# Retention scores of a macaron block: fp32 matmuls on four 32-row groups instead of hi/lo fp32r pairs

## The reference, cut to what matters

```python
x = x + 0.5 * ffn(layernorm(x))          # x is 1 x 1024 x 256
x = x + attn(layernorm(x))
x = x + 0.5 * ffn(layernorm(x))
# ffn: y = (silu(h @ gate * gs) * (h @ up * us)) @ down * ds, weights rounded to fp8, inner width 768
# attn: 16 heads of 16
q, k, v = split(h @ w_qkv)
q, k = xpos(q), xpos(k)                  # x * cos + rotate_every_two(x) * sin
scores = q @ k.T * D ** -0.5 * mask      # mask[h, t, s] = gamma_h ** (t - s) for t >= s, else 0
y = scores @ v
y = (y - mean) / sqrt(var + eps) * gn_weight + gn_bias      # over each head's 16 columns
out = (silu(h @ w_g) * y) @ w_proj
```

## Time and profile before

| | |
|---|---|
| three runs, us | 187.33, 188.22, 187.22; median 187.33 |
| span of the profiled execution | 187.8 us (its own time is not given apart from the span) |
| PE | 171.6 us busy, 91% |
| DVE | 142.9 us, 76% |
| ACT | 104.5 us, 56% |
| POOL | 62.9 us, 34% |
| PE clock granted, mean | 0.960 of full speed (1.0 is 2.4 GHz, 0.5 is 1.2 GHz) |

### The profile page before, as it was taken

One profiled execution on the slowest core, in us unless ns is written; L12 is line 12 of the kernel. 1 busy time (PEld: TensorE's weight loads), 2 busy tenths in 40 slices (PEclk: granted clock), 3 DMA queues, 4 the chain that ended last, 5 costly groups with the idle time before them and its releaser, 6 DMA issues.

```text
span 187.8 us, 3246 instructions
## 1 busy us (share of the span) xinstructions
PE 171.6 (91%) x1091; PEld 131.9 (70%) x1091; DVE 142.9 (76%) x302; ACT 104.5 (56%) x202; POOL 62.9 (34%) x68
## 2 busy tenths in 40 slices
PE   6745999899899999998999999999999999799992
PEld 2223867688878775866687777867677887588882
DVE  2899589999745486667796968878799899636664
ACT  3164199767208448584939576674926763224710
POOL 3535363353825210124161605215263915000000
PEclk9985599999999999999999999999999999889998
DMA  5898004403000000000000000000000000011002
GB/s 172 276 332 293 5 2 143 191 3 113 0 0 3 0 0 3 0 0 2 3 0 0 3 0 0 3 3 2 0 3 0 0 0 0 3 56 58 0 17 98
DMA packets 6848, 8.41 MB, mean 45 GB/s; under 512 B 416, under 2 KB 5552, under 8 KB 6832
## 3 DMA queue, kind: packets, MB, share of 16 engines
q1 hardware_dynamic: 6832, 8.20, 12.9%
HBM read 7.15 MB, written 1.05 MB: 44 GB/s over the span
## 4 chain that ended last, share of the span: by engine, by line
PE 36%; POOL 8%; DVE 7%; issue 5%; ACT 4%; POOLq 0%; DVEq 0%; ACTq 0%
PE bank L1017 12%; POOL grstd L326 6%; PE bank L1044 3%; PE bank L1121 3%; PE bank L1184 3%; PE bank L1141 3%; PE bank L1097 3%; PE bank L1070 2%; ACT fhi L451 2%; DVE rot L740 1%; PE bank L1134 1%; PE bank L1084 1%; PE bank L1081 1%; PE bank L1166 1%; DVE fuse L685 1%
## 5 line engine op out<-in xcount | busy, mean ns | idle before, releaser
L1017 PE MATMUL bank<-hh,gate_r 128*128 128x512 f32 x96 | 30.3, 436 | 4.7 <-DVE hh L669 2.3
L1017 PE MATMUL bank<-hh,up_r 128*128 128x512 f32 x96 | 28.0, 415 | 0.0
L398 ACT ACTIVATE gact<-bank,vec 128x512 f32<-128x512 f32 x24 | 16.4, 684 | 17.0 <-PE bank L1017 16.9
L1017 PEld LDWEIGHTS bank<-hh,gate_r 128*128 128x128 f32 x96 | 17.9, 202 | 11.2 <-issue 4.3
L1044 PE MATMUL bank<-down_r,fhi 128*128 128x256 f32 x96 | 25.1, 298 | 0.3 <-DVE flo L693 0.3
L326 POOL TENSOR_TENSOR grstd<-gve,neg_half 128x16 f32<-128x16 f32 x8 | 23.4, 2928 | 0.7
L1044 PE MATMUL bank<-down_r,flo 128*128 128x256 f32 x96 | 23.5, 282 | 0.0
L1017 PEld LDWEIGHTS bank<-hh,up_r 128*128 128x128 f32 x96 | 19.3, 201 | 4.7
L748 DVE TENSOR_TENSOR sc<-bank,msk 128x512 f32<-128x512 f32 x32 | 21.3, 682 | 0.7 <-PE bank L1121 0.7
L685 DVE SCALAR_TENSOR_TENSOR fuse<-bank,vec,gact 128x512 f32<-128x512 f32 x24 | 17.9, 744 | 3.8 <-PE bank L1017 3.6
L302 POOL TENSOR_SCALAR ve<-mv 128x1 f32<-128x1 f32 (+2 forms) x13 | 4.2, 321 | 49.1 <-DVE mv L630 49.1
(11 more groups left out here) (85 smaller groups left out, 346.1 us busy)
## 6 DMA issues: line engine op xcount, KB each, us to landing
raw<-in_rotation SPq DMA_DIRECT2D x1, 1536.0 KB, 6.5
xt<-in_L_attn_x SPq DMA_DIRECT2D x2, 512.0 KB, 4.6
out<-xt SPq DMA_DIRECT2D x8, 128.0 KB, 1.7
raw<-in_L_ffn_down_w SPq DMA_DIRECT2D x2, 384.0 KB, 7.5
wqkv<-in_L_attn_w_qkv SPq DMA_DIRECT2D x1, 768.0 KB, 9.4
raw<-in_rotation SPq DMA_DIRECT2D x1, 512.0 KB, 3.3
raw<-in_L_ffn_gate_w SPq DMA_DIRECT2D x1, 384.0 KB, 6.3
raw<-in_L_ffn_up_w SPq DMA_DIRECT2D x1, 384.0 KB, 6.9
```

Of the source, the lines that this page charges most:

```text
L398: nc.scalar.activation(gact[:, j % 2, :], pairs[j // (NG * NI)][j % 2][0][:, :], ACT.Silu, scale=gate_col[:, i:i + 1]).then_inc(silu_done, 1)
L1017: mm = pe.matmul(dst[:, :], wr[m][:, k * I + i * P:k * I + (i + 1) * P], half[:, k, g % NG, :], start=(k == 0 and half is hhi), stop=(k == ...
```

## The change

Scores become fp32 matmuls. Rotated q and k are transposed once (four 128 x 128 transposes into one bank). Of the transposed tile each 32 partitions hold two heads, so the score matmuls of 32 rows each take k's 32 partitions as weights and two masked copies of q as the moving side; row group r writes into bank 3 + r, all heads of it side by side, and one mask call evicts a bank. The state is summed in SBUF (`kvm` masked by DVE, `add_state` on POOL) in two slots, so that `b_kv` shares a bank with y. `group_mean` to `group_norm`, `gated` and `project_out` are reordered, and the roots on POOL with them. The core of the diff:

```diff
-        turn = [(bank[0], bank[1])] * 3 + [(bank[3], bank[4])]
-        pairs = [[(bank[2], bank[3]), (bank[4], bank[5])], [(bank[2], bank[5]), (bank[0], bank[1])]]
+        turn = [(bank[0], bank[1])] * 2 + [(bank[1], bank[2]), (bank[5], bank[6])]
+        pairs = [[(bank[2], bank[3]), (bank[4], bank[5])], [(bank[3], bank[4]), (bank[1], bank[2])]]
+        b_y, b_kv, b_qk, b_vg = bank[0][:, 0:C], bank[0][:, C:2 * C], bank[1], bank[2]
+        b_sc, b_gn = bank[3:7], bank[7]
+        b_qkT, b_turn = b_sc[0], b_sc[1]
...
+            def add_state(c):
+                pool.wait_ge(kvm_done, c + 1)
+                if c >= 2:
+                    pool.wait_ge(state_done, c - 1)
+                pool.wait_ge(y_half, KC * c)
+                pool.tensor_tensor(state[:, (c + 1) % 2], state[:, c % 2], kvm[:, :, :], ALU.add).then_inc(state_done, 1)
...
             for c in range(NT):
+                if c >= 2:
+                    group_roots(c - 2)
+                if 1 <= c < NT - 1:
+                    add_state(c)
                 if c + 3 < NT:
                     roots(NG + c + 3)
-                elif c == NT - 2:
-                    roots(NG + NT)
-                if c >= 1:
-                    group_roots(c - 1)
+            roots(NG + NT)
+            group_roots(NT - 2)
             group_roots(NT - 1)
...
+            def copy_qk(c):
+
+                act.wait_ge(qk_turned, c + 1)
+                if c >= 1:
+                    act.wait_ge(sc_done, c)
+                q_src, k_src = (b_qkT[:, a:a + C].rearrange("p (k t) -> p k t", k=KC) for a in (0, C))
+                nc.scalar.activation(kT[:, :, :], k_src, ACT.Copy)
+                for m in range(2):
+                    last = nc.scalar.activation(qM[:, :, m, :], q_src, ACT.Copy, scale=msk[:, 3 * P + m:3 * P + m + 1])
+                last.then_inc(qk_copied, 1)
+                if c >= 1:
+                    act.wait_ge(y_half, KC * c)
+                nc.scalar.activation(qT[:, :, :], q_src, ACT.Copy).then_inc(qT_copied, 1)
...
             for c in range(NT - 1):
+                if c >= 2:
+                    square(c - 2)
+                copy_v(c + 1)
+                if c >= 2:
+                    affine(c - 2)
                 if c + 2 < NT:
                     copy_h2(c + 2)
-                copy_qT(c)
-                split_qk(c + 1)
-                if c >= 2:
-                    affine(c - 2)
-                copy_k(c + 1)
-                copy_q(c + 1)
-                copy_v(c + 1)
-                if c >= 1:
-                    square(c - 1)
                 copy_y(c)
+                copy_qk(c + 1)
...
+            def mask_scores(c, r):
+
+                dve.wait_ge(sc_done, c + 1)
+                if c >= 1:
+                    dve.wait_ge(y_half, KC * c)
+                dve.tensor_tensor(sc[:, r].rearrange("p k m t -> p (k m) t"),
+                                  b_sc[r][:, :].rearrange("p (g t) -> p g t", t=P),
+                                  causal.unsqueeze(1).to_broadcast([P, 2 * KC, P]), ALU.mult).then_inc(sc_masked, 1)
...
             for c in range(NT - 1):
+                if c >= 2:
+                    group_mean(c - 2)
+                    group_var(c - 2)
                 rotate_parts(c + 1)
+                mask_kv(c)
                 mask_scores(c, 0)
-                rotate(c + 1)
                 mask_scores(c, 1)
+                if c >= 3:
+                    add_proj(c - 3)
                 if c >= 2:
                     group_norm(c - 2)
-                rest_qk(c + 1)
-                if c >= 2:
-                    gated(c - 2)
                 mask_scores(c, 2)
                 mask_scores(c, 3)
-                if c >= 2:
-                    add_proj(c - 2)
+                rotate(c + 1)
                 if c + 3 < NT:
                     norm_stats(NT + c + 3, NT + c + 4)
-
-                elif c == NT - 3:
-                    norm_stats(2 * NT, 2 * NT + 2)
                 elif c == NT - 2:
-                    norm_stats(2 * NT + 2, 2 * NT + TH)
-                if c >= 1:
-                    group_mean(c - 1)
+                    norm_stats(2 * NT, 2 * NT + TH)
+                if c >= 2:
+                    gated(c - 2)
                 if c + 3 < NT:
                     norm(NT + c + 3, NT + c + 4)
-                copy_state(c)
-                if 1 <= c < NT - 2:
-                    group_var(c - 1)
 
             c, j0 = NT - 1, NG * NI
-            mask_scores(c, 0)
+            group_mean(c - 2)
             group_var(c - 2)
             norm_tile(2 * NT)
+            norm_tile(2 * NT + 1)
+            mask_scores(c, 0)
             mask_scores(c, 1)
-            norm_tile(2 * NT + 1)
+            add_proj(c - 3)
+            group_norm(c - 2)
             mask_scores(c, 2)
+            mask_scores(c, 3)
             norm_tile(2 * NT + 2)
             norm_tile(2 * NT + 3)
-            mask_scores(c, 3)
-            group_norm(c - 2)
             rest_h(2, 0)
...
+            def scores(c):
...
+                pe.wait_ge(qk_copied, c + 1)
+                pe.wait_ge(qT_copied, c + 1)
+                pe.wait_ge(h2_done, min(c + 2, NT))
+                if c == 0:
+                    pe.wait_ge(fuse_done, NG * NI)
+                    pe.wait_ge(yd_done, NT - 1)
+                else:
+                    pe.wait_ge(sc_masked, HG * c)
                 for k in range(KC):
+                    for r in range(HG):
+                        at = slice(r * 2 * D, (r + 1) * 2 * D)
+                        mm = pe.matmul(b_sc[r][:, k * C:(k + 1) * C], kT[at, k, :],
+                                       qM[at, k].rearrange("p m t -> p (m t)"), start=True, stop=True)
                 mm.then_inc(sc_done, 1)
...
             turn_qk(0)
             down(6)
             project_qk(1)
+            update_state(0)
             down(7)
             for c in range(NT - 1):
+                scores(c)
+                if c >= 3:
+                    project_out(c - 3)
+                project_vg(c + 1)
+                if c >= 2:
+                    turn_gn(c - 2)
                 if c + 2 < NT:
                     turn_h2(c + 2)
+                values(c, 0)
+                values(c, 1)
+                if c >= 1:
+                    turn_y(c - 1)
                 turn_qk(c + 1)
                 if c + 2 < NT:
                     project_qk(c + 2)
+                if c + 1 < NT - 1:
+                    update_state(c + 1)
 
             c, j0 = NT - 1, NG * NI
+            scores(c)
+            project_out(c - 3)
+            turn_h(2)
             values(c, 0)
             values(c, 1)
             turn_y(c - 1)
             turn_gn(c - 2)
```

More of the change, by code:

```diff
@@ L71 @@
 FUSE_SLOTS = 4
+SG_SLOTS = 4
 WARM_UP = 5
@@ L151, in macaron @@
         rot = sb("rot", [P, 2, 2 * C])
[L152 to L154 removed]
+        qT = sb("qT", [P, KC, P])
+        qM = sb("qM", [P, KC, 2, P])
+        kT = sb("kT", [P, KC, P])
         v2 = sb("v2", [P, 2, H, 2 * D])
[L156 to L157 removed]
+        sc = sb("sc", [P, HG, KC, 2, P])
+        kvm = sb("kvm", [P, KC, P])
+        state = sb("state", [P, 2, KC, P])
         yT = sb("yT", [P, 2, KC, P])
@@ L879, in _ @@
             rotate(0)
-            rest_qk(0)
             tile_stats(NT + 2)
@@ L1101, in turn_qT @@
-            def turn_qT(c):
-                pe.wait_ge(q_copied, c + 1)
-                for k in range(KC):
-                    mm = pe.transpose(b_turn[:, C + k * P:C + (k + 1) * P], rot[:, c % 2, k * P:(k + 1) * P], ident)
-                mm.then_inc(qT_turned, 1)
-            def scores(c, g):
-                n = c * HG + g
-                if g == 0:
-                    pe.wait_ge(q_copied, c + 1)
-                    pe.wait_ge(k_copied, c + 1)
-                if n >= 2:
-                    pe.wait_ge(sc_masked, n - 1)
-                elif n == 0:
-                    pe.wait_ge(fuse_done, NG * NI)
-                    pe.wait_ge(silu_done, NG * NI)
-                for a in range(2):
-                    mm = pe.matmul(b_sc[g % 2][:, :], kk[:, c % 2, a, g, :], qM[c % 2][:, g].rearrange("p m t -> p (m t)"),
-                                   start=(a == 0), stop=(a == 1))
+                pe.wait_ge(rot_done, 2 * (c + 1))
@@ L1135, in values @@
                               skip_group_check=True)
-                for g in (2 * k, 2 * k + 1):
-                    pe.wait_ge(sc_masked, c * HG + g + 1)
-                    for m in range(HG):
-                        hd = g * HG + m
-                        r = (hd // 2 % 4) * 2 * D
-                        mm = pe.matmul(b_y[r:r + 2 * D, k * P:(k + 1) * P], v2[:, c % 2, hd, :], sc[:, g, m, :],
-                                       start=(c == 0 and hd % 2 == 0), stop=(hd % 2 == 1), skip_group_check=True)
+                for r in range(HG):
+                    pe.wait_ge(sc_masked, c * HG + r + 1)
+                    for m in range(2):
+                        hd = (k * HG + r) * 2 + m
```

(15 more changed lines are left out.)

188 lines of the change are left out of this document (64 added, 124 removed).

## The result

The changed kernel takes 190.72 us (median of four runs, 189.60 to 191.62) against 187.78 us for the kernel before (four runs, 187.22 to 188.40): a ratio of 1.0155 [1.0105, 1.0206], slower by 1.0 to 2.1%. The forecast was 184.8 us, faster.

A forecast was written before the change was run, and what follows sets the result against it. Before, a latency loop and PE's work tie at 10.65 us a chunk; after, DVE bounds it at 9.24. Span 187.8 less 4.75, plus 2.2 for the clock, is 185.25; less 0.47 gives 184.8 us, range 182.0 to 188.2.

The forecast's parts named there:

- 0.47 us (0.25%) above the median: Base of the sums: profiled span of 187.8 us against the median of 187.33; 0.47 taken off at the end.
- Scores: Eight fp32 score matmuls a chunk on PE, row groups overlapping like column groups: 1.2 us, ends 0.86 and 3.4.
- rival (a): Row groups overlap not or half, scores up to 3.4 us: 197.5 us; chance 0.06 above 187, 0.10 for 185.8 to 187.
- DVE already stands at its wait then ... so DVE should be first: Argument against rival (d): when the roots end, `group_norm` on DVE starts before POOL, which takes 0.07 us between instructions.
- rival (d): POOL's `add_state` blocks DVE's `group_norm` in c = 2 to 6, 5 x 0.9 = 4.5 us: 189.3 us; chance 0.05.
- DVE's order sets it: New chunk, c = 3 or 4: DVE's list sums to 9.24 us and bounds it, PE with 0.3 us of slack.
- centring and ACT's square 0.91: Step of DVE's chunk before the variance: 0.42 + 0.44 us and the hand-overs.
- The roots are off the loop: POOL's roots leave the chunk's chain of waits, because mean and variance move one chunk later.
- The stall: c = 7: `norm_tile(16)` waits for POOL's roots of tiles 16 to 19, behind `group_roots(5)`; DVE stands 4.7 us.
- The clock: After PE's gap in c = 7 the clock is low for values(7) and first `gate_up`: 2.2 us, ends 0 and 3.4.
- Rival (b): The clock stays at 2.4 GHz through c = 7: 182.6 us; chance 0.17.
- Rival (c): Hand layout too tight: unseen hand-overs add 0.4 us to each of seven chunks, 187.6 us, no change; chance 0.16.

The follow-up runs named there:

- both edits: Changed kernel with `add_state` waiting until `group_norm` is done and the roots of tiles 16 to 19 ahead of `group_roots(5)`: 184.52 us, 0.9778 to the kernel before.
- all edits but early statistics: On both edits, ACT's square ahead of the copy of qT and `group_norm` behind all four masks: 180.40 us, 0.9584 to the kernel before.

## Why the prediction was wrong

**Base.** "0.47 us (0.25%) above the median" compared a span with times. A run's time stands 2.1 us above its span for the kernel before (188.41 and 186.3) and 1.8 above it for the changed one (189.6 and 187.8). So the profiled execution took some 189.9 us, 2.1 above the median of 187.78. The two errors cancel: 187.78 less the forecast saving of span (2.55) and less 0.3 for the ends is 184.9. Measured between two events the miss is 5.0 us, whatever the base.

**Scores: right.** 1.2 us forecast from the column groups, 1.08 measured. Neither end of the range came up, and rival (a) falls. The second eight matmuls of the doubled scores take 0.86, so the two changes of shape around the score matmuls cost at most 0.22 us together; the forecast put them at 0.2. The Trainium skill (TensorE: Matmul & The Clock Gate, Measured speedup vs the span model) gives 3.07 for four row groups at 512 columns; the trace agrees with 3.2 at 256.

**The step that failed first: "DVE already stands at its wait then ... so DVE should be first".** In rival (d) I compared DVE's waiting with 0.07 us between two POOL instructions. But in the trace the next POOL instruction starts with the recorded end of the power (102.29, while the power ends at 102.33), and DVE comes 0.03 us after that end. "Then 0.34" for `group_norm` was 0.86 start to start. The condition of the rival was right ("If POOL goes first in c = 2 to 6"), the chance 0.05 was not; its price, 5 x 0.9, was too high, since the norm waits only for the rest of the other's 0.73 us: 5 x 0.52 = 2.6. By the Trainium skill (SBUF — State Buffer, Summary: rules for kernel authors) when VectorE has two inputs in SBUF and GpSimd reads SBUF too, whoever issues second waits for the first to finish; the trace agrees, with the norm ending 0.28 and 0.29 us behind `add_state` in two kernels. With that rule I should have asked which of the two issues first, from the rows, before giving 0.05.

**The second: "DVE's order sets it".** I walked through DVE's list once round and took the sum, 9.24, as the chunk. Two gaps inside it were not DVE's: "centring and ACT's square 0.91" was 1.16, since the square stands behind `copy_qk` on ACT, and "aggregate to `norm` 1.17" was 1.29. Together with the norm's 0.52 they make 10.13, which is the chunk, but the sum over a list says nothing about which gap counts. The experiments do: doubling the scores (0.86 us more PE) costs nothing in c = 2 to 5, taking a tile's statistics earlier costs instead of giving, moving the square gives 0.24. The bound is the loop in which "values 1.25" were 1.63, and in which the copies of q and k lie ahead of the square. I had written that "The roots are off the loop"; they are its longest link, because the loop closes through the square's place on ACT. Of the 4.8 us missed ahead of the last stretch, 2.6 are the collision and 2.2 this loop: with both edits DVE's start of c = 7 is at 62.52 after the first scores, against 60.3. The first trace shows it already. From c = 5 to 6, where no tile is left to norm, I took its items off DVE's list (8.4 us), but DVE then waits 1.09 us for `turn_y` and 1.28 for the square, and variance to variance stays 10.13 us (108.76 to 118.89).

**The stall: right.** 4.7 forecast, 4.63 measured; the kernel before with late roots shows it alone, at 6.0 us with what follows it. I had booked it as time given back, without asking what it would be worth to avoid it: 3.5 us for one line moved.

**The clock: right in place, a little high.** 2.2 us forecast, 1.76 measured by keeping PE busy. Rival (b) falls for this kernel.

Rival (c), a layout too tight by 0.4 us a chunk, had the size of the loop's part (0.9 us in c = 3 and 4, less 0.52 for the collision) though not its mechanism, and had 0.16. With (c)'s 2.8 us and 2.6 for the collision the forecast would have been 190.2. The range ended at 188.2 because the far side of (c) and (d) were each left out; they came together.

Left open: why the clock fell in PE's first wait in one execution and in its second in another, and why the square ahead of the copy gave more time than its shorter chunks explain. The loop through `affine` is read from three traces; no run was made to test it.

## What to carry to other kernels

Look for the longest closed loop of waits, not the sum of one engine's list: write the loop down across engines, back to its own start, and for each link ask whether it is data or only an order in a list. When such an order is changed, draw the loop again: the late norm opened a new one through `affine`. When work moves to GpSimd, look at what runs there just ahead of it and whom that releases: here the next GpSimd instruction and the released VectorE instruction started within 0.07 us, both with two inputs in SBUF, and the released one took 0.94 us instead of 0.42. When a call moves in an engine's list, ask for every call behind it what it now waits for; here one line in POOL's list was worth 3.5 us, and with the orders put right the change that cost 1.6% (1.3% when measured again) became one that gives 4.2% [3.8, 4.5]. Whether the same orders would help the kernel before was not tried.

## What the hardware did that I had not expected

- `group_norm` beside `add_state` took 0.94 us instead of 0.42; with `add_state` behind it 0.43. In the kernel with all edits but early statistics `add_state` (from 100.67) met `rotate` (from 100.35 and 100.69) instead and took 1.04 us itself where it takes 0.73, while both parts of `rotate` kept 0.42 and 0.43: the loser is not always the same engine.
- A second set of eight fp32 score matmuls on four row groups added 0.86 us to the 1.08 of the first.
- In `turn_h(2)` PE of the changed kernel waits twice, 3.64 us to 134.65 and 2.53 (in the second execution 2.94) to 138.26. The clock fell inside the first wait in one execution and inside the second in the other; both times it was back near 143 us.
